# 111 unread products of the identity between the steps of a fixed TensorE order, in a Mamba, attention and gated-FFN tower on one core

## The chip, the core and the metric

The kernel runs on one core of a Trainium2 chip. The core has TensorE (PE in the profile, with its weight loads as PEld), VectorE (DVE), ScalarE (ACT), GpSimd (POOL) and SyncE (SP), which here only starts transfers. The metric is the device time of one execution in microseconds. The kernel before took 393.94 us as the median of three runs (392.65 to 394.93).

## What is computed

Sixteen sequences of 128 tokens go through an embedding of width 192, two Mamba layers, one attention layer and one feed-forward layer, each with a residual sum. Cut to its core:

```python
x = emb[input_ids]
for i in range(2):                       # Mamba, inner width 384, 16 states
    xr, res = split(rmsnorm(x) @ in_proj_w[i])
    xr = silu(causal_conv4(xr) + conv_b[i])
    dt, Bm, Cm = split(xr @ x_proj_w[i])
    delta = softplus(dt @ dt_proj_w[i] + dt_proj_b[i])
    y = selective_scan(xr, delta, -exp(A_log[i]), Bm, Cm, D[i])
    x = x + (y * silu(res)) @ out_proj_w[i]
q, k, v = split(layernorm(x) @ w_qkv)    # 12 heads of 16
attn = relu(1 + qk + qk ** 2 / 2); attn = attn / sum(attn)
x = x + (attn @ v) @ w_proj + b_proj
up, gate = split(quant(rmsnorm(layernorm(x))) @ ternary(w_in).T)
x = x + quant(rmsnorm(silu(gate) * up)) @ ternary(w_out).T
```

## The kernel before

**Staging.** The two Mamba layers are cut into eight chunks j = 0 to 7: four groups of four sequences, and two layers. Each chunk has 512 tokens and three channel blocks c of 128. Chunk 4 is the first of layer 1. Attention and the feed-forward part run by sequence, s = 0 to 15.

**Order.** Nothing is scheduled at run time. Each engine has a list of calls, written out by hand, and walks through it in order. Semaphores tie the lists together: a call waits for the count that its data or its bank needs. On TensorE the list of calls begins behind the helper functions, with turn_in(0, 0).

**TensorE's helpers.** turn_in(j, k) (L972) transposes the normalised input of a chunk, eight 128x128 pieces in two calls. project_in(j, q) (L983) and project_rest(j, q) (L989, L991) form the input projection, in three parts q, which ScalarE's first_tap and silu_gate_in (L374) read. project_x(j) (L998) gives the rows of dt, B and C, which ScalarE's take_xp copies to dbl (L328). project_steps(j) (L1005) gives the step sizes, which ScalarE reads for the softplus. spread_b(j) (L1010) and spread_cg(j) (L1016, L1018) spread B, C and their product over the partitions, for VectorE. project_out(j, b) (L1065) is the output projection, which VectorE's add_h (L2335) adds to h. Behind them come turn_x, project_qk, project_v, scores(s) (L1115), values(s) (L1127), turn_sums(s) (L1135, L1138), turn_attention and project. In the feed-forward part turn_input (L1160), project_up (L1167), turn_hidden(s) (L1174) and project_down(s) (L1181) stand. project_down(s) waits for ScalarE's copy of the turned tile (take_hidden, L534), and VectorE's add_ffn(s) (L2459) waits for it and makes the last sum of a sequence, which SP stores.

**Flags.** Whether a chunk's states need the long form is decided at run time. VectorE counts and writes a flag (L2328); every engine reads it, TensorE in states_pe(j) (L1021 and after), and takes a branch. In this run every chunk takes the short branch, in which states_pe only raises a semaphore. ScalarE's take_xp(j) waits for that semaphore of chunk j - 2.

**Banks.** PSUM has eight banks of 128x512 float32, and tables at the head of the file say which bank each call writes. A product that nobody reads has to find its bank free, so it may stand only behind the count that says that the last reader of the bank is done.

**What is not used.** The helper keep_clock(n, b) (L965) is defined in the kernel before and called nowhere:

```python
def keep_clock(n, b):
    for _ in range(n):
        nc.tensor.matmul(bank[:, b, 0:P], ident[:, :], ident[:, :], start=True, stop=True)
```

## Time and profile before

| | |
|---|---|
| median of the runs | 393.94 us |
| the profiled execution | 396.22 us |
| its span, first to last instruction | 394.2 us |
| mean granted TensorE clock | 0.908 of full |
| PE busy | 325.8 us (83%) |
| DVE busy | 294.0 us (75%) |
| ACT busy | 272.4 us (69%) |
| POOL busy | 235.3 us (60%) |

The profile is of one execution, which has its own time. The busy shares are means over stages that differ: the Mamba layers fill about the first 236 us, attention and the feed-forward part the rest. The clock is given as a share of full: 1.00 is 2.4 GHz and 0.50 is 1.2 GHz. A plain float32 product shows as two MATMUL records, a transpose as one.

### The profile page before, as it was taken

To read this page: it belongs to the slowest core of one execution; us is meant where nothing else is said; L and a number is where in the kernel's file an instruction comes from. 1 tells how busy PE (TensorE), PEld (TensorE's weight loads), DVE (VectorE), ACT (ScalarE), POOL (GpSimd) and SP (SyncE) were. 2 spreads that over 40 slices of the span, in tenths; PEclk is the share of its full clock that TensorE was granted. 3 is DMA by queue.
4 is the path that set the end of the run, shared out by engine and by line. 5 is a ranking of instruction groups with operands and counts; after the bars stand their busy time and mean duration, and the time that the engine had idled before them with its cause. 6 is when DMAs were issued, how large, how long until landed. Compare 5 with 4: busy or idle time off the path is not lost. (4 is left out here: it accounts for less than half of the span.)

```text
span 394.2 us, 6391 instructions
## 1 busy us (share of the span) xinstructions
PE 325.8 (83%) x1794; PEld 188.7 (48%) x1794; DVE 294.0 (75%) x636; ACT 272.4 (69%) x552; POOL 235.3 (60%) x316
## 2 busy tenths in 40 slices
PE   0199965768978899998989889988998899899955
PEld 0143422254425534364335558646765646477633
DVE  3019999899899899999998959941365737467874
ACT  2459999696688998799876964353555547566852
POOL 6751168578819459296392691760134836678893
PEclk9999995959899998998979969998999969899976
DMA  6891000000000000000000000000000000000111
GB/s 151 150 274 23 1 2 0 2 1 0 2 1 1 2 0 2 2 1 0 2 1 0 1 3 2 0 2 2 0 2 2 0 2 1 2 12 10 32 60 50
DMA packets 7134, 7.87 MB, mean 20 GB/s; under 512 B 1643, under 2 KB 6138, under 8 KB 7098
## 3 DMA queue, kind: packets, MB, share of 16 engines
q1 hardware_dynamic: 5464, 5.71, 4.9%
q0 software_dynamic: 768, 1.57, 2.8%
q8 instruction: 15, 0.25, 0.2%
q10 hardware_dynamic: 866, 0.17, 0.2%
q14 instruction: 21, 0.17, 0.2%
HBM read 5.87 MB, written 1.57 MB: 19 GB/s over the span
## 5 line engine op out<-in xcount | busy, mean ns | idle before, releaser
L983 PE MATMUL bank<-ring,win 128*128 128x512 f32 x96 | 53.4, 690 | 7.4 <-DVE dmin L2248 3.3
L1856 POOL TENSOR_TENSOR arena<-arena 128x512 f32<-128x512 f32 x24 | 34.0, 1428 | 39.9 <-DVE arena L2282 25.9
L2239 DVE SCALAR_TENSOR_TENSOR pair<-bank,cw,pair 128x508 f32<-128x508 f32 (+2 forms) x72 | 49.8, 733 | 5.8 <-issue 4.7
L1838 POOL TENSOR_TENSOR arena<-arena,dl 128x512 f32<-128x512 f32 x24 | 31.9, 1332 | 22.9 <-DVE dl L2231 22.6
L1065 PE MATMUL bank<-wout,pair 128*128 128x192 f32 x192 | 37.7, 352 | 3.3 <-ACT ring L382 3.3
L480 ACT ACTIVATE du<-bank 128x512 f32<-128x512 f32 x48 | 25.3, 597 | 19.9 <-PE bank L1115 17.4
L1065 PEld LDWEIGHTS bank<-wout,pair 128*128 128x128 f32 x192 | 34.1, 206 | 9.5 <-ACT ring L382 3.7
L1844 POOL TENSOR_TENSOR du<-dl,pair 128x512 f32<-128x512 f32 x24 | 33.1, 1383 | 8.8 <-DVE dmin L2248 8.8
L983 PEld LDWEIGHTS bank<-ring,win 128*128 128x128 f32 x96 | 19.0, 216 | 35.0 <-issue 18.8
L2269 DVE TENSOR_TENSOR_SCAN arena<-arena 128x512 f32<-128x512 f32 x24 | 34.8, 1461 | 0.3
L972 PE MATMUL bank<-ident,ring 128*128 128x128 f32 x64 | 11.7, 330 | 23.8 <-ACT ring L409 19.0
L1850 POOL TENSOR_TENSOR pair<-pair,arena 128x512 f32<-128x512 f32 x24 | 31.2, 1316 | 0.0
L989 PE MATMUL bank<-ring,win_rest 64*128 64x512 f32 x48 | 26.3, 641 | 0.0
L991 PE MATMUL bank<-ring,win_rest 64*128 64x512 f32 x48 | 26.3, 641 | 0.0
L998 PE MATMUL bank<-pair,wx 128*125 128x512 f32 x48 | 24.0, 639 | 1.3 <-issue 1.3
L972 PEld LDWEIGHTS bank<-ident,ring 128*128 128x128 f32 x64 | 8.9, 170 | 30.1 <-issue 23.5
L1890 POOL TENSOR_TENSOR pair<-pair,gout 128x512 f32<-128x512 f32 x16 | 20.5, 1285 | 1.8 <-PE bank L1174 1.1
L335 ACT ACTIVATE pair<-bank,cb,cw 128x512 f32<-128x512 f32 x24 | 18.5, 787 | 3.8 <-PE bank L991 2.3
L1833 POOL TENSOR_TENSOR rstd<-ms,neg_half 128x4 f32<-128x4 f32 x8 | 9.2, 1147 | 19.7 <-DVE ms L2219 16.5
L1167 PE MATMUL bank<-wq,arena 96*128 96x512 bf16 x64 | 18.6, 397 | 1.4 <-ACT arena L507 1.4
L2263 DVE TENSOR_TENSOR arena<-du,bank 128x512 f32<-128x512 f32 x24 | 16.2, 681 | 4.3 <-PE bank L1010 2.8
L2277 DVE TENSOR_TENSOR arena<-du,bank 128x512 f32<-128x512 f32 x24 | 16.3, 678 | 4.1 <-POOL pair L1850 3.5
(177 smaller groups left out, 887.1 us busy)
## 6 DMA issues: line engine op xcount, KB each, us to landing
out<-h SPq DMA_DIRECT2D x16, 96.0 KB, 1.6
win<-in_w SPq DMA_DIRECT2D x2, 384.0 KB
arena<-ffn_in_t SPq DMA_DIRECT2D x1, 768.0 KB
wout<-out_w SPq DMA_DIRECT2D x2, 288.0 KB
win_rest<-in_w SPq DMA_DIRECT2D x2, 192.0 KB
arena<-ffn_out_t SPq DMA_DIRECT2D x1, 384.0 KB
wa<-w_qkv SPq DMA_DIRECT2D x1, 384.0 KB
h<-emb,idx POOLq DMA_INDIRECT x16
```

The costliest lines, as they stand in the source:

```text
L480: nc.scalar.activation(sq[s % 2][:, r, :, :], bank[:, SC_BANKS[s][r], :].rearrange("p (j n) -> p j n", j=JH), ACT.Square, scale=HD ** -0.5 ...
L983: nc.tensor.matmul(bank[:, IN_BANKS[j][m], :], win[:, j // NG, m * P:(m + 1) * P], xtr[:, j % 2, i, :], start=True, stop=False)
L989: nc.tensor.matmul(bank[:, IN_BANKS[j][2 * q], :], rest[64:P, :], xtr[64:P, j % 2, 1, :], start=False, stop=True).then_inc(x_ready if 2 * ...
L991: nc.tensor.matmul(bank[:, IN_BANKS[j][2 * q + 1], :], rest[0:64, :], xtr[0:64, j % 2, 0, :], start=False, stop=True).then_inc(x_ready if ...
L998: last = nc.tensor.matmul(bank[0:XM, XP_BANKS[j], :], wx[:, j // NG, c, :], xc[:, j % NG, c, :], start=(c == 0), stop=(c == CI - 1))
L1065: last = nc.tensor.matmul(bank[:, O_BANKS[j][b], i * D:(i + 1) * D], xc[:, j % NG, c, t0:t0 + LEN], wout[:, j // NG, c, :], start=(c == 0) ...
L1838: nc.gpsimd.tensor_tensor(relu_s[:, c, :], relu_s[:, c, :], dl[:, j % NG, c, :], ALU.subtract).then_inc(rest_done, 1)
L1844: nc.gpsimd.tensor_tensor(du[:, g, c, :], dl[:, g, c, :], xc[:, g, c, :], ALU.mult).then_inc(du_ready, 1)
L1850: nc.gpsimd.tensor_tensor(xc[:, j % NG, c, :], sz[:, j % NG, c, :], yv[:, c, :], ALU.mult).then_inc(gated, 1)
L1856: nc.gpsimd.tensor_tensor(yv[:, c, :], yv[:, c, :], bx[:, c, :], ALU.add).then_inc(yv_done, 1)
L2239: nc.vector.scalar_tensor_tensor(acc, seqs(bank[:, IN_BANKS[j][c], :])[:, :, 0:LEN - tap], cw[:, j // NG, c, TAPS - 1 - tap:TAPS - tap], a ...
L2269: nc.vector.tensor_tensor_scan(bx[:, c, :], da[:, c, :], bx[:, c, :], 0.0, ALU.mult, ALU.add).then_inc(scan_done, 1)
```

## The change

keep_clock is called at 19 places of TensorE's list, with 111 products in all. The numbers of products are 7, 1, 1, 1, 4, 6, 10, 4, 4, 6, 8, 2, 1, 2, 4, 4, 3, 25 and 18. Each writes 128 columns of a bank that no one reads before it is written again. Before most of them stands the wait that says the bank is free. Some of these waits stood a few calls further on before and are moved ahead, others are new. No call changes its place against the others, on any engine.

```diff
             turn_in(0, 0)
             turn_in(0, 1)
+            keep_clock(7, 2)
             pe.wait_ge(xt_ready, 2)
             project_in(0, 0)
...
             project_in(1, 1)
+            pe.wait_ge(conv[0], 3)
+            keep_clock(1, 1)
             project_rest(1, 1)
             pe.wait_ge(sz_ready, 2)
-            pe.wait_ge(conv[0], 3)
             project_in(1, 2)
...
             project_in(2, 0)
+            pe.wait_ge(sz_ready, 6)
+            keep_clock(1, 1)
             project_rest(2, 0)
-            pe.wait_ge(sz_ready, 6)
             project_x(1)
...
             project_in(2, 1)
+            pe.wait_ge(conv[0], 9)
+            keep_clock(1, 6)
             project_rest(2, 1)
+            pe.wait_ge(delta_ready, 1)
+            keep_clock(4, 0)
             pe.wait_ge(conv[1], 9)
-            pe.wait_ge(delta_ready, 1)
-            pe.wait_ge(conv[0], 9)
             project_steps(1)
...
             project_in(2, 2)
+            pe.wait_ge(delta_ready, 5)
+            keep_clock(6, 0)
             pe.wait_ge(bx_ready, 3)
             turn_in(3, 0)
...
             states_pe(0)
             pe.wait_ge(flag_ready, 1)
+            keep_clock(10, 4)
             pe.wait_ge(xt_ready, 7)
             pe.wait_ge(p_done, 3)
             project_steps(2)
...
             states_pe(1)
+            pe.wait_ge(delta_ready, 8)
+            keep_clock(4, 1)
             pe.wait_ge(p_done, 6)
             turn_in(4, 0)
...
             states_pe(4)
+            pe.wait_ge(p_done, 13)
+            pe.wait_ge(p_done, 14)
             pe.wait_ge(p_done, 15)
+            keep_clock(4, 3)
             pe.wait_ge(t_ready, 15)
             pe.wait_ge(sz_ready, 18)
             project_steps(5)
...
             project_out(4, 1)
+            pe.wait_ge(sz_ready, 20)
+            keep_clock(6, 0)
             pe.wait_ge(h_added, 9)
             turn_in(7, 0)
             pe.wait_ge(h_added, 10)
             turn_in(7, 1)
-            pe.wait_ge(sz_ready, 20)
             project_x(6)
+            pe.wait_ge(delta_ready, 18)
+            keep_clock(8, 5)
             pe.wait_ge(t_ready, 18)
             pe.wait_ge(bx_ready, 18)
-            pe.wait_ge(delta_ready, 18)
             project_steps(6)
...
             project_rest(7, 0)
+            pe.wait_ge(sz_ready, 21)
+            keep_clock(2, 4)
             pe.wait_ge(flag_ready, 6)
-            pe.wait_ge(sz_ready, 21)
             project_in(7, 1)
+            pe.wait_ge(p_done, 16)
+            pe.wait_ge(p_done, 17)
+            pe.wait_ge(p_done, 18)
+            keep_clock(1, 1)
             project_rest(7, 1)
             states_pe(5)
             pe.wait_ge(delta_ready, 19)
-            pe.wait_ge(p_done, 18)
+            keep_clock(2, 3)
             project_in(7, 2)
...
             states_pe(6)
             pe.wait_ge(k_out, 2)
+            keep_clock(4, 5)
             pe.wait_ge(q_out, 4)
             pe.wait_ge(p_done, 21)
             scores(0)
...
             turn_hidden(10)
+            pe.wait_ge(y_done, 14)
+            keep_clock(4, 2)
             pe.wait_ge(qxt_ready, 16)
             project_up(15, 1)
             pe.wait_ge(y_done, 15)
             project_up(15, 0)
+            keep_clock(3, 2)
             pe.wait_ge(yt_ready, 11)
             project_down(10)
             pe.wait_ge(sg_ready, 16)
             turn_hidden(11)
+            pe.wait_ge(h_out, 9)
+            keep_clock(25, 1)
             pe.wait_ge(yt_ready, 12)
             project_down(11)
             pe.wait_ge(h_out, 11)
             turn_hidden(12)
+            pe.wait_ge(y_done, 16)
+            keep_clock(18, 0)
             pe.wait_ge(yt_ready, 13)
             turn_hidden(13)
```

On TensorE, at the end of its list, these rows stand in the kernel before. L1160 and L1174 are turn_input and turn_hidden, L1167 is project_up and L1181 project_down:

```order
L1160 MATMUL bank<-ident,ring 96x128 x2
L1174 MATMUL bank<-ident,pair 128x128 x4
L1167 MATMUL bank<-wq,arena 128x512 x4
L1181 MATMUL bank<-wq,arena 128x192 x4
L1174 MATMUL bank<-ident,pair 128x128 x4
L1181 MATMUL bank<-wq,arena 128x192 x4
L1174 MATMUL bank<-ident,pair 128x128 x8
L1181 MATMUL bank<-wq,arena 128x192 x4
```

At the same place of the changed kernel:

```order
L1160 MATMUL bank<-ident,ring 96x128 x2
L1174 MATMUL bank<-ident,pair 128x128 x4
L967 MATMUL bank<-ident 128x128 x4
L1167 MATMUL bank<-wq,arena 128x512 x4
L967 MATMUL bank<-ident 128x128 x3
L1181 MATMUL bank<-wq,arena 128x192 x4
L1174 MATMUL bank<-ident,pair 128x128 x4
L967 MATMUL bank<-ident 128x128 x25
L1181 MATMUL bank<-wq,arena 128x192 x4
L1174 MATMUL bank<-ident,pair 128x128 x4
L967 MATMUL bank<-ident 128x128 x18
L1174 MATMUL bank<-ident,pair 128x128 x4
```

The 25 products stand between turn_hidden(11) and project_down(11), and the 18 part turn_hidden(12) from turn_hidden(13), which were one row of eight transposes.

On TensorE, behind the branch of states_pe(1) and before turn_in(4, 0) (L972) and project_in(3, 2) (L983):

```order
 L1043 COMPARE_AND_BRANCH
 L1026 UNCONDITIONAL_BRANCH
+L967 MATMUL bank<-ident 128x128 x4
 L972 MATMUL bank<-ident,ring 128x128 x4
 L983 MATMUL bank<-ring,win 128x512 x2
```

The four products come after the branch, so the transposes stand one row further from it. The same form stands behind states_pe(0), (4), (5) and (6).

## Rows read from the trace of the kernel before

**Rows 1.** The page's slices: busy tenths of the span's 40 equal parts.
```profile
PE   0199965768978899998989889988998899899955
...
DVE  3019999899899899999998959941365737467874
...
PEclk9999995959899998998979969998999969899976
```

**Rows 2.** Waits of DVE, 28 to 232 us: total, times, longest.
```profile
DVE arena L2263 <- PE bank L1010: 2.8, 2, 1.8
DVE h L2335 <- PE bank L1065: 2.2, 2, 1.6
```

**Rows 3.** Timeline of PE in attention: start us, us, line, operation, idle before.
```profile
238.60 0.83 PE L1138 MATMUL bank<-ident,arena 128*128 128x128 f32 x6
239.27 0.81 PE L1135 MATMUL bank<-dl,ones 128*128 128x384 f32 x2
```

**Rows 4.** Timeline of PE at the kernel's end.
```profile
377.23 1.02 PE L1167 MATMUL bank<-wq,arena 96*128 96x512 bf16 x4 [0.95 <-ACT arena L507]
378.95 0.49 PE L1181 MATMUL bank<-wq,arena 128*128 128x192 bf16 x4 [0.70 <-ACT arena L534]
379.74 1.09 PE L1174 MATMUL bank<-ident,pair 128*128 128x128 f32 x4 [0.29 <-DVE pair L2453]
383.24 0.80 PE L1181 MATMUL bank<-wq,arena 128*128 128x192 bf16 x4 [2.41 <-ACT arena L534]
...
386.92 1.09 PE L1174 MATMUL bank<-ident,pair 128*128 128x128 f32 x4 [2.03 <-DVE pair L2453]
...
389.77 0.60 PE L1174 MATMUL bank<-ident,pair 128*128 128x128 f32 x4
```

**Rows 5.** The last piece of the chain that ended last.
```profile
391.77 0.42 DVE h L2459
```

**Rows 6.** Timeline at the start, PE and ACT.
```profile
20.00 5.84 PE L983 MATMUL bank<-ring,win 128*128 128x512 f32 x8 [0.82 <-ACT ring L382]
...
26.97 2.12 ACT L335 ACTIVATE pair<-bank,cb,cw 128x512 f32<-128x512 f32 x3 [1.20 <-PE bank L991]
...
28.62 3.68 PE L983 MATMUL bank<-ring,win 128*128 128x512 f32 x8
```

**Rows 7.** Timeline of PE behind states_pe(1).
```profile
99.21 0.87 PE L972 MATMUL bank<-ident,ring 128*128 128x128 f32 x4 [2.12 <-issue]
```

**Rows 8.** Timeline of PE and ACT behind states_pe(0).
```profile
77.54 0.69 ACT L328 ACTIVATE dbl<-bank,one_rows 125x512 f32<-125x512 f32 x1 [2.21 <-PEq L1025]
...
78.37 1.53 PE L1005 MATMUL bank<-dbl,wdt 29*128 29x512 f32 x6 [2.65 <-ACT dbl L328]
...
84.21 6.62 PE L1065 MATMUL bank<-wout,pair 128*128 128x192 f32 x24 [3.26 <-ACT ring L382]
...
85.52 1.18 ACT L364 ACTIVATE bank<-bank 128x512 f32<-128x512 f32 x2 [0.87 <-DVE dl L2231]
```

**Rows 9.** Timeline of PE behind states_pe(6), scores(0) and scores(1).
```profile
225.28 1.14 PE L1115 MATMUL bank<-pair 32*128 32x256 f32 x12 [0.26 <-issue]
228.22 1.20 PE L1115 MATMUL bank<-pair 32*128 32x256 f32 x12 [1.80 <-ACT du L480]
```

**Rows 10.** Timeline of PE in chunks 6 and 7.
```profile
183.48 1.12 PE L972 MATMUL bank<-ident,ring 128*128 128x128 f32 x8 [1.97 <-DVE h L2335]
184.44 4.43 PE L998 MATMUL bank<-pair,wx 128*125 128x512 f32 x6
189.74 1.13 PE L1005 MATMUL bank<-dbl,wdt 29*128 29x512 f32 x6 [0.87 <-ACT dbl L328]
```

**Rows 11.** Stretches: length, busy PE, PEld, DVE, ACT, POOL, clock, DMA share, GB/s.
```profile
79.00:89.20 10.20, 6.94 (x26) 5.71 (x21) 10.13 (x16) 8.89 (x17) 7.98 (x6) 0.50 0.00 1
...
229.20:236.00 6.80, 6.67 (x68) 3.82 (x64) 3.22 (x8) 4.15 (x8) 6.80 (x6) 0.50 0.01 4
379.40:389.60 10.20, 5.46 (x27) 4.52 (x27) 7.03 (x18) 2.74 (x6) 8.52 (x19) 0.50 0.13 41
```

More of the change, by code:

```diff
@@ L1245, in _ @@
             count_short(0)
-            pe.wait_ge(delta_ready, 5)
             project_x(2)
@@ L1277, in _ @@
             pe.wait_ge(flag_ready, 2)
-            pe.wait_ge(delta_ready, 8)
             project_in(3, 2)
@@ L1794, in _ @@
             project_down(12)
-            pe.wait_ge(y_done, 16)
             turn_hidden(14)
```

## The prediction

> **What bounds the kernel now.** I read the view of the slices first. The reader is to see two halves [rows 1]: up to slice 24 (some 236 us) VectorE stands at 9 nearly everywhere, and TensorE has open slices; from there TensorE stands at 8 or 9 and VectorE falls back. The clock line shows 5 in five slices and 6 to 8 in several more. So a slow TensorE costs time at full rate only in the second half; in the first it costs time where VectorE waits for TensorE. Those waits are few: of 204 us, VectorE waited 2.8 us for the spread of B (L1010) and 2.2 us for the output projection (L1065), in two waits each [rows 2]. The third place is the end, where TensorE, ScalarE and VectorE alternate and each instruction is on the path [rows 4]. The profiled execution took 396.22 us, with a span of 394.2; the median shown is 393.94. I work out differences in the execution and add them to the median.
>
> **The price of one product.** keep_clock issues plain float32 products of 128x128. The nearest row is the one of turn_sums, three products of the same shape that show as six records: from its start at 238.60 to the next line's at 239.27 are 0.67 us, so 0.111 a record and 0.222 us a product at the full clock [rows 3]. Four float32 transposes show as four records: 0.60 us at the full clock and 1.09 at the half [rows 4], not far from double. So I take a record at half clock as 0.222 and a product as 0.44 us.
>
> **The end of the kernel.** This is the heaviest term. turn_hidden(11) starts at 379.74, and project_down(11) starts at 383.24 after 2.41 idle; turn_hidden(13) starts at 386.92 after 2.03 idle [rows 4]. The change puts 25 products into the first gap and 18 into the second: 5.55 and 4.00 us at the full clock against 4.44 us of idle in all. The waits put ahead of them (h_out 9, y_done 16) do not hold them back: VectorE runs add_ffn(8) and hidden(15) well before, since the square of tile 15 and the copy of tile 11 on ScalarE, for which project_down(11) waited, come after hidden(15). So the products start as soon as TensorE gets to them. The 4 and 3 products a little earlier (0.9 and 0.7 us) fit the gaps there of 0.95 and 0.70 [rows 4], and I cost them at nothing. With these, I expect the clock, which fell at about 379.4, to stay full. Then the walk, in times of before: turn_hidden(11) is issued by 380.2; 25 products to 385.7; project_down(11) and turn_hidden(12), 0.35 + 0.45, to 386.5; 18 products to 390.5. The rounds of the last hidden tiles, which were what TensorE waited for at 386.92, are then all done: project_down(11) is 2.5 late and VectorE's add behind it too, but its rounds for 13, 14 and 15 follow by about 389.7. From turn_hidden(13) to the end of the last add were 5.27 us (386.92 to 392.19), mostly at half clock. At full clock: 0.45 for turn_hidden(13) (four records of 0.11), 0.35 for project_down(12) (0.49 with its tail), 0.45 for turn_hidden(14), 0.8 for the wait for ScalarE's copy of tile 13 and project_down(13), 0.45 for turn_hidden(15), 0.7 and 0.2 of latency for the copy of tile 15, and 0.49 and 0.42 for the last product and add [rows 4, 5]: some 4.2 us. End at 394.7 against 392.19: **+2.6**. Who waits: SP's last stores, one for one. Without the gain in clock it would be +3.6. If the clock does not hold and the 25 start at half rate, say thirteen of them, it is 13 x 0.22 = 2.9 more.
>
> **The start.** Seven products stand between turn_in(0,1) and project_in(0,0). In between TensorE was idle 0.82 us, and it worked below the full rate then: the eight records of project_in took 5.84 us, 0.73 each, against 3.68 for eight at 28.62 [rows 6], though the clock column, which starts with its first event, says full. ScalarE's first tap waited 1.20 us for the products behind them [rows 6], and VectorE starts behind it, so this is on the path. At half rate the seven are 3.1 us, 2.3 more than the gap. The activity may raise the clock earlier: by one early change, project_in ends 0.6 before; with none, 0.9 after. I take -0.3, nearer the first, since the gap was the one break in TensorE's work there.
>
> **After the flags.** Three of the groups stand behind states_pe, where TensorE's sequencer reads a flag and branches. The idle time is spent in that read, and the products come after it. So they fill nothing there.
> - Before turn_in(4,0): 2.12 idle, put down to "issue" [rows 7]. Four products are 0.9 us. Behind stands spread_b(2), for which VectorE waited the longest of its waits for that line, 1.8 us [rows 2]; this passes on in full: **+0.9**. If the clock held, project_in(3,2) would give back 1.4, so -0.5; at half clock +1.7.
> - Before project_steps(2): ten products are 2.2 us, and TensorE waited 2.65 us there for ScalarE's dbl [rows 8], and ScalarE itself had waited for TensorE's branch until 77.54 [rows 8]. Only 0.8 lies between branch and steps, so project_steps(2) comes 1.4 late. ScalarE has 0.87 to spare behind it, at 85.52 [rows 8], so **+0.5**. Between -0.3 (the output projection at 84.21, 6.62 us at half clock, runs faster and the shorter of the two waits for it, 0.6, goes [rows 2, 8]) and +1.5.
> - Before scores(0): 0.26 idle [rows 9] against 0.9 for four products: **+0.65**. Here TensorE bounds from now on. The real gap, 1.80 us, lies behind scores(0), where ScalarE squares [rows 9], and gets no product.
>
> **Chunk 6 and 7.** Six products before turn_in(7,0) fit the 1.97 idle, with 0.6 to spare [rows 10]. There the clock fell right behind, and project_x(6) took 4.43 us, nearly all at half rate [rows 10]: at full rate 1.6 come back, somewhat under the 2.2 that half of it would be. The eight products before project_steps(6) are 1.8 us in a gap of 0.87 [rows 10], so 0.9 is taken again: **-0.6**; +0.9 if the clock falls all the same. Five more products (1.1 us) stand in front of and between the projections of chunk 7, at 193 to 197, with no idle time; the break before spread_b(6), in which the clock fell again, takes them up. They may keep the clock for spread, turn_x and project_out(5,0), behind which VectorE had its longest wait for the output projection, 1.6 us [rows 2]. Only part of this break is filled, so I count **-0.3**, between 0 and -1.6.
>
> **What else moves.** Waits were taken forward so that a bank is free: conv[0] 3 and 9, sz_ready 6 and 20, delta_ready 1, 5, 8, 18, 19. The one with work behind it is delta_ready 5 with six products before turn_in(3,0), where TensorE had no gap: project_rest(2,2) and the gate's silu on ScalarE come 1.3 late, but ScalarE waits 2.21 us a little later for the flag's branch, which covers it [rows 8]. conv[0] 9 holds project_rest(2,1) for some 0.5 us, ahead of 1.35 idle. The single products there are 0.2 each beside the same covers. Four before project_steps(5), behind a branch too, delay it by some 0.7, and ScalarE loads a table and takes a tap before it needs it. All at nothing; up to +1.0 if these covers fail.
>
> **Sum:** -0.3 + 0.9 + 0.5 + 0.65 - 0.6 - 0.3 + 2.6 = +3.45 us. 393.94 + 3.45 = **397.4 us**.
>
> **Rivals.**
> 1. The clock holds nearly everywhere beside the products, and TensorE's faster work carries. The places are the half-clock stretches of 79 to 89, 229 to 236 and 379 to 389 [rows 11] and the waits of VectorE [rows 2]. For: the falls follow breaks such as those of 2.65, 2.12, 1.97 and 1.80 us [rows 7 to 10]. Against: the products at scores(0) and turn_in(4,0) are not in the break. Price: the 6.7 us of TensorE at half clock in 229 to 236, where it bounds, give 3.3; VectorE's waits for L1065 give 2.2, and that at spread_b(2) 1.4 [rows 2]: -6.9, against 2.6 at the end and 2.2 in products: -2.1, and with 0.6 at the start -2.7, so 391.2. It decides for faster once more than 4.8 us come back; the stretch of scores alone is most of that. 8%. The Trainium skill ("TensorE: Matmul & The Clock Gate", section "Terms") reckons the penalty of throttled time as that time x (1 - K/N), so half of it. By that rule the 27.2 us of the three stretches would be worth 13.6 us, and the time 380; the rows speak against it, since VectorE was busy 10.1 of the 10.2 us from 79 to 89 [rows 11], and I leave it 1 of the 8%.
> 2. The 25 products run largely at half rate and the clock follows late: +2.9 on the sum, or the covers above fail too: 400.0 to 401. 12%.
> 3. A product costs what a transpose does, one record, 0.111 us. 25 are 2.8 against 2.41, 18 are 2.0 against 2.03: the end costs +0.4 less 1.0 of regained clock, and the places behind the flags half: some -0.3 in all, 393.6. Against: turn_sums shows two records a product [rows 3]. Or the early terms turn out as gains of 1.5 to 2: then some 394 to 395.5. Together 18%.
> 4. The forecast, 395.5 to 399.5: 62%.
>
> **Numbers.** The range reaches from 393.5 to 400.3: it leaves out rival 1 and half of rival 2. Over 0.5% (2 us, about what a measurement can tell) means above 395.9 or below 392.0: slower 0.70 (the forecast less its lowest part, and rival 2), faster 0.08, same 0.22.
>
> **What would show it.** Right: the 25 and 18 rows of L967 last some 5.5 and 4 us; project_down(11) follows them without a wait, and so does turn_hidden(13); the clock is full from 379 on and the last add ends 2 to 3 us later, counted from turn_hidden(11). At turn_in(4,0) some 2 us of idle stand ahead of the products still. Wrong: a wait for y_rounded between the 18 products and turn_hidden(13), as then the price is off; or no half clock in 229 to 236.

## The result and the profile after

The changed kernel takes 398.06 us (median of four runs, 397.26 to 399.79) against 393.84 for the kernel before beside it. The ratio is 1.0114, with a 95% interval of 1.0069 to 1.0158: 4.5 us more, with bounds of 2.7 and 6.2. The forecast was 3.45 more, 397.4. In comparisons of single terms below, I use ratios to the kernel before; 0.001 is 0.39 us. A ratio leaves out executions that are more than 1.5% above the fastest of their kernel.

The page of the changed kernel: span, busy times, and the same slices as [rows 1].

```profile
span 395.8 us, 6828 instructions
...
PE 340.0 (86%) x2016; PEld 211.9 (54%) x2016; DVE 295.3 (75%) x636; ACT 272.1 (69%) x552; POOL 235.8 (60%) x316
...
PE   0299985969879788999989979988998899899996
...
PEclk9999995978898999999998969999899989999999
```

TensorE is busy 14 us longer than before (340.0 against 325.8) and its mean clock rose from 0.908 to 0.948, while VectorE, ScalarE and GpSimd did the same work as before. A better clock and a longer time stand side by side; the rest of this text is about why. The profiled execution took 397.81 us, only 1.6 more than the one profiled before (396.22). That pair understates the difference, since that execution of before was longer than all four of its timed runs (392.65 to 394.93).

**The end.** TensorE's timeline (start us, us, line, operation, records, idle before), which answers to [rows 4]:

```profile
378.72 0.63 PE L1174 MATMUL bank<-ident,pair 128*128 128x128 f32 x4 [0.29 <-DVE pair L2478]
379.19 5.75 PE L967 MATMUL bank<-ident 128*128 128x128 f32 x50
384.77 0.49 PE L1181 MATMUL bank<-wq,arena 128*128 128x192 bf16 x4
385.10 0.60 PE L1174 MATMUL bank<-ident,pair 128*128 128x128 f32 x4
385.54 4.18 PE L967 MATMUL bank<-ident 128*128 128x128 f32 x36
389.56 0.60 PE L1174 MATMUL bank<-ident,pair 128*128 128x128 f32 x4
...
392.82 0.49 PE L1181 MATMUL bank<-wq,arena 128*128 128x192 bf16 x4 [0.54 <-ACT arena L534]
```

The 25 products are 50 records in 5.75 us, the 18 are 36 in 4.18, and what follows each has no idle time in front. TensorE has become the bound of this piece. From turn_hidden(11) at 378.72 to the end of the last add (393.35 and 0.42 us, the same add as in [rows 5]) are 15.05 us; before they were 12.45, from 379.74 to 392.19 [rows 4, 5]. Four transposes now take 0.60 us where most took 1.09. Counted from start to start, the 25 take 5.58 us (379.19 to 384.77) and the 18 take 4.02, so 0.223 us a product; the lengths of the rows, 5.75 and 4.18, contain the tail of the last product.

**Behind the flags.** The same timeline behind states_pe(0), (1) and (6), which answers to [rows 7 to 9]:

```profile
77.83 2.50 PE L967 MATMUL bank<-ident 128*128 128x128 f32 x20
80.26 1.13 PE L1005 MATMUL bank<-dbl,wdt 29*128 29x512 f32 x6
...
85.74 7.03 PE L1065 MATMUL bank<-wout,pair 128*128 128x192 f32 x24 [3.76 <-ACT ring L382]
...
100.89 1.25 PE L967 MATMUL bank<-ident 128*128 128x128 f32 x8 [1.87 <-issue]
101.94 1.06 PE L972 MATMUL bank<-ident,ring 128*128 128x128 f32 x4
102.79 3.10 PE L983 MATMUL bank<-ring,win 128*128 128x512 f32 x4
...
226.37 1.16 PE L967 MATMUL bank<-ident 128*128 128x128 f32 x8
227.46 1.14 PE L1115 MATMUL bank<-pair 32*128 32x256 f32 x12
...
230.42 1.14 PE L1115 MATMUL bank<-pair 32*128 32x256 f32 x12 [1.82 <-ACT du L480]
```

Before turn_in(4,0) the idle time is still there (1.87 us, put down to "issue"), and the four products come behind it, as extra. Before scores(0) they are 1.1 us in front of a call that had waited 0.26. The real gap, 1.82 us before scores(1), is untouched. VectorE's waits for TensorE, of the stretch that [rows 2] shows (L2288 and L2360 are L2263 and L2335 of before), grew in sum. The first for the output projection went from 0.66 to 1.80 us; the second, for a later chunk, shrank from 1.56 to 1.30.

```profile
DVE arena L2288 <- PE bank L1010: 4.2, 2, 2.5
DVE h L2360 <- PE bank L1065: 3.1, 2, 1.8
```

**Chunk 6.** Here the products are in the gap of [rows 10]:

```profile
183.78 1.50 PE L967 MATMUL bank<-ident 128*128 128x128 f32 x12
185.91 1.12 PE L972 MATMUL bank<-ident,ring 128*128 128x128 f32 x8 [0.62 <-DVE h L2360]
186.86 2.74 PE L998 MATMUL bank<-pair,wx 128*125 128x512 f32 x6
189.44 1.95 PE L967 MATMUL bank<-ident 128*128 128x128 f32 x16
191.32 1.14 PE L1005 MATMUL bank<-dbl,wdt 29*128 29x512 f32 x6
```

0.62 us of the wait for h are left over, so nothing is pushed back, and project_x(6) takes 2.74 where it took 4.43 [rows 10]. That this gain is owed to the products is not shown: in the trace of waits_only (below), which issues no product, the call takes 2.74 too, behind 2.00 us idle.

```profile
182.70 2.74 PE L998 MATMUL bank<-pair,wx 128*125 128x512 f32 x6
```

The eight that follow overrun the gap of 0.87 us, as costed.

**The clock.** Stretches as in [rows 11]: length, busy time of each engine, clock (third from the end). The stretch of scores is still at half, and the last 16.6 us are at nearly full clock:

```profile
231.50:238.30 6.80, 6.54 (x68) 3.72 (x67) 2.99 (x2) 4.27 (x9) 6.80 (x5) 0.50 0.01 4
379.40:396.00 16.60, 13.27 (x122) 12.57 (x120) 7.17 (x19) 4.05 (x7) 7.32 (x18) 0.98 0.14 42
```

**Where the time came in.** I set VectorE's instructions of the two traces side by side, one by one. The changed kernel is 0.47 us later at 61 us, 0.8 at 85, 1.9 at 91 (behind the wait for the output projection of chunk 0) and 2.6 at 106 (behind spread_b(2)). It then falls back to 1.7 at 196 and 1.4 at 212, is 2.1 later at 233, just behind scores(0), and takes its last 2.6 in the end. Between 288 and 349 it goes from 2.3 later to 1.0 earlier, where the change has no product: the half clock there held 3.4 us from 317 where it had held 6.8 from 314, and one of 3.4 at 342 was absent. The trace of waits_only (below), which has no product, shows the falls of the changed kernel there, 3.4 us from 313 and none at 342, so I count nothing of this to the change. The same caution holds for the first half: VectorE of waits_only, with no product at all, is 2.35 us earlier than that of the kernel before at 104 us, where half clock is absent at 99.5, and 5.1 earlier at the end. One pair of traces is therefore no measure of a term below some 2 us.

### The profile page after: what moved, and what is told of

Its sections match the earlier page's. It is cut to its first block and busy times, and to the rows that moved or that the text cites. A ratio compares the mean times of both kernels' runs of the same rounds, so it can differ in the third digit from the quotient of the medians.

```text
span 395.8 us, 6828 instructions
## 1 busy us (share of the span) xinstructions
PE 340.0 (86%) x2016; PEld 211.9 (54%) x2016; DVE 295.3 (75%) x636; ACT 272.1 (69%) x552; POOL 235.8 (60%) x316
## 3 DMA queue, kind: packets, MB, share of 16 engines
q0 software_dynamic: 768, 1.57, 2.8%
HBM read 5.87 MB, written 1.57 MB: 19 GB/s over the span
## 5 line engine op out<-in xcount | busy, mean ns | idle before, releaser
L983 PE MATMUL bank<-ring,win 128*128 128x512 f32 x96 | 51.2, 665 | 7.0 <-DVE dmin L2273 3.3
L1065 PE MATMUL bank<-wout,pair 128*128 128x192 f32 x192 | 39.2, 361 | 3.9 <-ACT ring L382 3.8
L1065 PEld LDWEIGHTS bank<-wout,pair 128*128 128x128 f32 x192 | 35.4, 212 | 10.0 <-issue 4.1
L967 PEld LDWEIGHTS bank<-ident 128*128 128x128 f32 x222 | 29.3, 207 | 11.1 <-issue 6.9
L983 PEld LDWEIGHTS bank<-ring,win 128*128 128x128 f32 x96 | 18.4, 209 | 31.3 <-issue 19.8
L967 PE MATMUL bank<-ident 128*128 128x128 f32 x222 | 31.3, 295 | 2.1 <-issue 1.9
L1875 POOL TENSOR_TENSOR pair<-pair,arena 128x512 f32<-128x512 f32 x24 | 33.0, 1390 | 0.0
L972 PE MATMUL bank<-ident,ring 128*128 128x128 f32 x64 | 10.5, 306 | 20.3 <-ACT ring L409 19.0
L998 PE MATMUL bank<-pair,wx 128*125 128x512 f32 x48 | 22.2, 599 | 1.3 <-issue 1.3
L972 PEld LDWEIGHTS bank<-ident,ring 128*128 128x128 f32 x64 | 8.0, 156 | 24.1 <-issue 19.5
L2288 DVE TENSOR_TENSOR arena<-du,bank 128x512 f32<-128x512 f32 x24 | 16.1, 678 | 5.7 <-PE bank L1010 4.2
```

Of the source, the lines that this page charges most:

```text
L983: nc.tensor.matmul(bank[:, IN_BANKS[j][m], :], win[:, j // NG, m * P:(m + 1) * P], xtr[:, j % 2, i, :], start=True, stop=False)
L1065: last = nc.tensor.matmul(bank[:, O_BANKS[j][b], i * D:(i + 1) * D], xc[:, j % NG, c, t0:t0 + LEN], wout[:, j // NG, c, :], start=(c == 0) ...
L1875: nc.gpsimd.tensor_tensor(xc[:, j % NG, c, :], sz[:, j % NG, c, :], yv[:, c, :], ALU.mult).then_inc(gated, 1)
```

## The experiments

Each kernel ran against the kernel before on the same chip. There were three groups of kernels, each on a chip of its own: waits_only, tail_only, no_tail and no_behind_flags; tail_fit, ahead_of_flags, scores_gap and in_the_gaps; and the remaining four. The tables give the ratio with its 95% interval, the span and mean clock of the profiled execution, and the **last piece**, from turn_hidden(11) to the end of the last add.

### Taking the change apart

Theory: three lots of products carry it, the 25 and 18 at the end, the five groups behind the flags (10, 4, 4, 2, 4), and the other 44, which together pay a little. Rival: the moved waits cost, or the shared effect of the clock does.

waits_only keeps every wait of the change and no product:

```diff
             pe.wait_ge(h_out, 9)
-            keep_clock(25, 1)
...
             pe.wait_ge(y_done, 16)
-            keep_clock(18, 0)
```

> The changed kernel with all 111 products left out and only its moved and added waits kept. Theory (the products cost TensorE's time where its idle time is shorter than they are, the waits cost nothing): within 0.5 us of the kernel before, ratio 0.999 to 1.001. Rival (the waits taken forward hold back project_rest and what stands behind it): 1 us or more slower. Second rival (the clock's luck decides): no statement, anywhere within 1.5 us.

tail_only keeps, with the waits, only the last four groups:

```diff
-            keep_clock(7, 2)
...
-            keep_clock(4, 5)
...
             keep_clock(4, 2)
...
             keep_clock(3, 2)
...
             keep_clock(25, 1)
...
             keep_clock(18, 0)
```

> Only the last four groups of products (4, 3, 25 and 18) are kept, with all waits of the change. Theory: TensorE becomes the bound of the last 13 us; +2.6 us against the kernel before, ratio 1.0066; in the profile from the start of turn_hidden(11) to the end of the last add some 15.0 us, where 12.45 stood. Rival (the cost sits in the Mamba layers): +0 to +0.5.

no_tail is the changed kernel without the last two:

```diff
-            keep_clock(25, 1)
...
-            keep_clock(18, 0)
```

> The changed kernel without the groups of 25 and 18; the other 68 products stay. Theory: 2.6 us less than the changed kernel, so +1.0 to +1.8 against the kernel before (ratio 1.003 to 1.0045); the piece from turn_hidden(11) to the last add takes 11.5 to 12.45 us, less than before if the 4 and 3 products keep the clock up. Rival: as slow as the changed kernel.

no_behind_flags is the changed kernel without the five groups behind branches:

```diff
-            keep_clock(10, 4)
...
-            keep_clock(4, 1)
...
-            keep_clock(4, 3)
...
-            keep_clock(2, 3)
...
-            keep_clock(4, 5)
```

> The changed kernel without the five groups that stand behind a read flag (10, 4, 4, 2 and 4 products). Theory: they stand behind the idle time and not in it, and cost 0.9 at turn_in(4,0), 0.5 to 1.4 at project_steps(2) and 0.65 at scores(0): about 2.0 to 2.4 us less than the changed kernel, so +1.5 to +2.2 against the kernel before (ratio 1.004 to 1.0055). Rival (what they do to the clock outweighs their time): no less than the changed kernel, or more.

neither leaves both out, so 44 products stay (the two edits above in one):

> The changed kernel without the five groups behind the flags and without the 25 and 18 at the end; 44 products stay. Theory (the flags' groups and the end are the whole cost): no slower than the kernel before, ratio 0.997 to 1.001. Rival (the products in the dense stretches of chunks 1, 2, 6 and 7 and at the start cost too): 1 us slower or more.

| kernel | ratio | 95% | span, clock | last piece |
|---|---|---|---|---|
| waits_only | 0.9996 | 0.9973 to 1.0019 | 389.1, 0.924 | 12.59 |
| tail_only | 1.0023 | 0.9997 to 1.0048 | 393.9, 0.935 | 15.05 |
| no_tail | 1.0078 | 1.0046 to 1.0110 | 397.0, 0.927 | 13.37 |
| no_behind_flags | 1.0017 | 0.9993 to 1.0042 | 391.6, 0.948 | 15.05 |
| neither | 0.9957 | 0.9927 to 0.9988 | 400.9, 0.905 | 12.94 |

The profiled execution of neither took 402.77 us, while its other twelve took 390.13 to 393.84, so its last two columns do not stand for the kernel.

The moved waits cost nothing that can be measured. Four of the kernels make a square, in us against the kernel before (394 times the ratio less one):

| | without 25 and 18 | with them |
|---|---|---|
| without the groups behind flags | -1.7 | +0.7 |
| with them | +3.1 | +4.5 |

The end costs 2.4 in the upper row and 1.4 in the lower. The groups behind flags cost 4.8 in the left column and 3.8 in the right. Each of the four has an interval of 1 to 2 us to either side, so that the two columns differ is not shown. The kernel neither comes from another chip than no_tail and no_behind_flags. A third pair, tail_only less waits_only, prices the last four groups at 1.1 us.

The other products can be priced within one group of kernels: no_behind_flags is tail_only with 37 products more, those at the start and in chunks 1, 2, 6 and 7. Their ratios, 1.0017 and 1.0023, and medians, 394.62 and 394.55 us, are the same. So these 37 cost nothing and bring nothing that can be told, within some 1.4 us.

Two of the traces also show where the groups behind the flags cost. VectorE of the changed kernel, set against VectorE of no_behind_flags, is 0.8 us later at 86 us, 2.6 at 92.8 (behind the wait for the output projection of chunk 0) and 4.9 at 108.5 (behind spread_b(2)); from 160 to 212 it is 3.8 to 4.1 later, 5.3 at 233, and 4.2 from 239 to the end. The whole cost of this pair arises before 110 us, at the first two flags, and nothing is lost in attention. no_tail against waits_only shows the same steps: 2.5 us by 92 and 4.7 by 108. The rows of no_behind_flags, against the output projection at 85.74, turn_in(4,0) at 101.94 and the wait of 2.5 us above:

```profile
84.35 5.78 PE L1065 MATMUL bank<-wout,pair 128*128 128x192 f32 x24 [3.96 <-ACT ring L382]
...
98.40 0.63 PE L972 MATMUL bank<-ident,ring 128*128 128x128 f32 x4 [2.00 <-issue]
98.86 1.88 PE L983 MATMUL bank<-ring,win 128*128 128x512 f32 x4
...
103.56 0.69 DVE L2283 TENSOR_TENSOR arena<-du,bank 128x512 f32<-128x512 f32 x1 [0.25 <-PE bank L1010]
```

At both places the clock adds to the products' own time. The output projection takes 7.03 us where it takes 5.78 here, and the first part of project_in(3,2) 3.10, in a stretch at 0.50 from 101.8 to 105.2, where it takes 1.88 at full clock. Whether the four products brought that second fall is not shown: the kernel before has it too, at 99.5, and so has tail_only, while waits_only has none there.

The last piece explains part of the end's two prices: without the products it is 12.5 us in waits_only but 13.37 in no_tail, because the half clock lasted longer in it there. What the products add to the piece is therefore 2.5 or 1.7, as the execution falls. tail_only came out at +0.9 where I had expected the whole 2.6. Its last piece is 15.05, exactly as expected; what gave back the rest lies before turn_hidden(11), and no run isolates it.

no_tail was a miss of mine. I had written +1.0 to 1.8 and it was +3.1, and this is the first sign that the groups behind the flags had been costed too low. no_behind_flags missed too, on the other side (+1.5 to +2.2 expected, +0.7 measured).

### The end, with products that fit

The timeline gives a product 0.22 to 0.23 us. If the 25 and 18 cost because they overrun gaps of 2.41 and 2.03 us [rows 4], then 10 and 8 should pay.

```diff
             pe.wait_ge(h_out, 9)
-            keep_clock(25, 1)
+            keep_clock(10, 1)
...
             pe.wait_ge(y_done, 16)
-            keep_clock(18, 0)
+            keep_clock(8, 0)
```

The rest is as in tail_only.

> The waits of the change, and at the end of the kernel groups of 4, 3, 10 and 8 products instead of 4, 3, 25 and 18; no others. At 0.222 us each, 10 and 8 are 2.2 and 1.8 us, in gaps of 2.41 and 2.03. Theory (the cost at the end is products beyond the gap, and the clock they hold is worth 1 us): the piece from turn_hidden(11) to the last add takes 11.2 to 11.6 us, against 12.45 before and 15.05 with 25 and 18; ratio 0.997 to 0.999 against the kernel before, 2.5 to 3.5 us faster than with 25 and 18. Rival (a product costs what a transpose does, so 25 and 18 fit as well): no difference from the run with 25 and 18.

The ratio is 0.9952 (0.9924 to 0.9981), a little better than expected; span 390.3, clock 0.934, last piece 11.58. TensorE's timeline of its end:

```profile
376.72 0.63 PE L1174 MATMUL bank<-ident,pair 128*128 128x128 f32 x4 [0.29 <-DVE pair L2463]
377.19 2.40 PE L967 MATMUL bank<-ident 128*128 128x128 f32 x20
380.22 0.49 PE L1181 MATMUL bank<-wq,arena 128*128 128x192 bf16 x4 [0.64 <-ACT arena L534]
...
380.99 1.95 PE L967 MATMUL bank<-ident 128*128 128x128 f32 x16
383.90 0.63 PE L1174 MATMUL bank<-ident,pair 128*128 128x128 f32 x4 [0.96 <-DVE pair L2463]
```

And the same end in waits_only, without products:

```profile
374.46 1.09 PE L1174 MATMUL bank<-ident,pair 128*128 128x128 f32 x4 [0.30 <-DVE pair L2459]
377.96 0.80 PE L1181 MATMUL bank<-wq,arena 128*128 128x192 bf16 x4 [2.41 <-ACT arena L534]
...
381.64 1.08 PE L1174 MATMUL bank<-ident,pair 128*128 128x128 f32 x4 [2.03 <-DVE pair L2459]
```

The waits for ScalarE and VectorE are back as the bound, but short (0.64 and 0.96), so no product is on the path, and the transposes, here 0.63, stay at the full clock's duration. From turn_hidden(11) to turn_hidden(13) are 7.18 us in both: the gain lies behind, where the clock is full (3.46 us from turn_hidden(13) to the start of the last project_down, against 4.47). 25 products fewer at the two places are 7 parts in 1000, or 2.8 us, against tail_only (each ratio from its own chip), and the two last pieces differ by 3.47.

### Ahead of a flag or behind it

The claim that products behind a flag fill nothing, because the idle time is spent in the read, has a counterpart: products ahead of the read should hide in it.

```diff
+            pe.wait_ge(xt_ready, 7)
+            keep_clock(8, 1)
             states_pe(0)
             pe.wait_ge(flag_ready, 1)
...
-            states_pe(1)
             pe.wait_ge(delta_ready, 8)
+            keep_clock(6, 1)
+            states_pe(1)
```

The edit is against waits_only, so no other product is issued.

> The waits of the change, and products at two flags only, ahead of the flag's read and not behind it: eight before states_pe(0), six before states_pe(1). Theory (behind a flag the idle time is already over, ahead of it the products fill it): turn_in(4,0) starts no more than 2.2 us behind the last projection as before, the products hide, the clock holds in one of the two stretches behind, and VectorE's waits for L1065 and L1010 shrink: 0 to 1.5 us faster than the kernel before. Rival (the read of the flag waits until TensorE's products are through, so products push it wherever they stand): 1.5 to 3 us slower.

The ratio is 0.9986 (0.9954 to 1.0017), span 390.1, clock 0.924, last piece 12.56. TensorE's timeline:

```profile
76.70 2.05 PE L967 MATMUL bank<-ident 128*128 128x128 f32 x16
...
96.93 1.61 PE L967 MATMUL bank<-ident 128*128 128x128 f32 x12
98.90 0.63 PE L972 MATMUL bank<-ident,ring 128*128 128x128 f32 x4 [0.37 <-issue]
```

The six stand in the former break, of which 0.37 us are left, and turn_in(4,0) starts at 98.90 where it started at 99.21 [rows 7]. In waits_only, without products, it starts at 98.32 behind 1.96 us of idle. Four products cost 1.1 us behind the branch, and six are hidden ahead of it. The rival, by which products push the read wherever they stand, is out: 1.5 to 3 us slower was its price. The kernel gains nothing measurable either.

Two kernels price the groups behind the branch alone. ten_at_steps2 has every wait and only the ten (the cuts here are against waits_only):

```diff
             states_pe(0)
             pe.wait_ge(flag_ready, 1)
+            keep_clock(10, 4)
             pe.wait_ge(xt_ready, 7)
```

> The waits of the change, and only the ten products before project_steps(2), behind the read of flag 0. The prediction priced them at +0.5. Its changed trace shows VectorE's wait for the output projection of chunk 0 at 1.80 us where 0.66 stood, and its shift growing there by 1.9 in all. Theory now: +1.5 to +2.0 us against the kernel before, ratio 1.004 to 1.005. Rival (the price of the prediction): +0.5, ratio 1.001.

fours_behind_flags has only the four before turn_in(4,0) and the four before scores(0):

```diff
             pe.wait_ge(delta_ready, 8)
+            keep_clock(4, 1)
             pe.wait_ge(p_done, 6)
...
             pe.wait_ge(k_out, 2)
+            keep_clock(4, 5)
             pe.wait_ge(q_out, 4)
```

> The waits of the change, and only the four products before turn_in(4,0) and the four before scores(0), both behind a flag. Theory: 0.9 and 0.65, each on the path: +1.5 us, ratio 1.004. Rival (one of the two is taken up by a later wait): +0.9 or less.

| kernel | ratio | 95% | span, clock | last piece |
|---|---|---|---|---|
| ten_at_steps2 | 1.0040 | 1.0006 to 1.0074 | 392.9, 0.916 | 12.54 |
| fours_behind_flags | 1.0147 | 1.0095 to 1.0200 | 398.8, 0.914 | 13.01 |

The ten cost 1.6 us by the ratio, with bounds of 0.2 and 2.9, so the ratio alone does not exclude the 0.5 of the prediction. The traces speak more clearly: from 75 to 92 us VectorE falls back by 1.4 to 2.8 us against the kernel before in the three that have the ten there (the changed kernel, no_tail, ten_at_steps2), and by 0.6 at most in each of the others, without them. TensorE's and VectorE's timeline of ten_at_steps2, to be held against [rows 8]:

```profile
77.22 4.13 PE L967 MATMUL bank<-ident 128*128 128x128 f32 x20 [1.00 <-issue]
...
86.77 6.42 PE L1065 MATMUL bank<-wout,pair 128*128 128x192 f32 x24 [3.76 <-ACT ring L382]
...
93.22 0.56 DVE L2342 TENSOR_TENSOR h<-h,bank 128x384 f32<-128x384 f32 x1 [1.20 <-PE bank L1065]
```

Here the ten ran at half clock (4.13 us), and the output projection starts at 86.77, where it started at 84.21. VectorE, which I had not counted on this path, waits 1.20 us for it instead of 0.66 in the kernel before.

The fours cost 5.8 us (3.7 to 7.9, from six executions), far above what their places can show: in the changed kernel four products take 1.05 us before turn_in(4,0) and 1.09 before scores(0). It is also more than the +3.1 of no_tail, which has the same fours and 60 products more. In the profiled execution VectorE is 1.7 us later than that of the kernel before at 98 us, ahead of the first product, 2.3 at 233 and 4.5 at the end. The last part came where the kernel has no product, with stretches of half clock and TensorE fully busy, of which these are two:

```profile
268.40:271.80 3.40, 3.40 (x16) 2.93 (x18) 1.23 (x5) 1.00 (x3) 0.30 (x1) 0.51 0.00 0
...
343.40:350.20 6.80, 6.78 (x30) 4.25 (x30) 2.59 (x7) 3.04 (x6) 3.06 (x8) 0.51 0.00 0
```

Four transposes take 1.09 us at half clock and 0.60 at full, so by an estimate such a stretch of 3.4 us costs 1.5 where TensorE is the bound. That the fours bring these stretches about is not shown. The long profiled execution of neither, which has no product behind a flag, has stretches of the same lengths at nearly the same places (from 267, 304, 321 and 345 us, against 268, 302, 319 and 343 here). The first of them:

```profile
267.00:273.80 6.80, 6.48 (x26) 5.38 (x26) 2.52 (x9) 1.75 (x4) 1.78 (x4) 0.50 0.01 4
```

And the changed kernel has the same fours, with fewer such stretches. So the 5.8 us are no price of the fours, and their cause stays open.

### The gap that the change left open

scores_gap puts six products into the 1.80 us before scores(1) [rows 9], and none elsewhere. Theory: the clock holds over 229 to 236, where TensorE bounds, and some 3 us come back.

```diff
             pe.wait_ge(v_out, 2)
+            keep_clock(6, 1)
             scores(1)
```

> The waits of the change, and one group of six products between scores(0) and scores(1), in the gap of 1.80 us where TensorE waits for ScalarE's squares. Theory: the 1.3 us fit, the clock holds from 229 to 236, where TensorE bounds, and 2 to 3 us come back; ratio 0.993 to 0.996. Rival (the clock falls all the same, as the score products do not count for it): within 0.5 us of the kernel before; or the wait for v_out 2 comes later than I read it, and it is 0.5 slower.

The ratio is 1.0050 (1.0017 to 1.0083), span 393.0, clock 0.917, last piece 13.35. TensorE's timeline and the stretches:

```profile
226.76 1.61 PE L967 MATMUL bank<-ident 128*128 128x128 f32 x12 [0.30 <-DVE dmin L2255]
...
231.26 1.14 PE L1115 MATMUL bank<-pair 32*128 32x256 f32 x12 [0.98 <-ACT du L480]
```

```profile
229.00:236.00 7.00, 6.02 (x86) 3.81 (x83) 4.30 (x11) 4.71 (x10) 7.00 (x6) 1.00 0.00 1
...
377.10:390.80 13.70, 8.65 (x43) 6.54 (x41) 8.30 (x21) 4.16 (x8) 8.61 (x19) 0.51 0.16 50
```

The first half of the theory held. The clock stands at 1.00 from 229 to 236, scores(2) takes 1.14 us where it takes 2.08 in waits_only, and VectorE, set against waits_only, gained 2.5 us over it (the profiled execution of waits_only was its fastest). The second half fell: the half clock came back at 298, 339 and for 13.7 us at 377 (10.2 before [rows 11]), and the kernel is 2 us slower. The mean clocks of its executions, 0.916 to 0.926, are hardly above those of the kernel before beside it, 0.902 to 0.924. That the six products moved the falls from one place to others is an argument from one trace and not shown.

### All gaps together

in_the_gaps joins what fitted: 8 and 6 products ahead of the flags, 6 before turn_in(7,0), 3 (not 8) before project_steps(6), 6 before scores(1), and 4, 3, 10 and 8 at the end, 54 in all. gaps_but_scores is the same without the six before scores(1). Against waits_only:

```diff
+            pe.wait_ge(xt_ready, 7)
+            keep_clock(8, 1)
             states_pe(0)
...
-            states_pe(1)
             pe.wait_ge(delta_ready, 8)
+            keep_clock(6, 1)
+            states_pe(1)
...
+            keep_clock(6, 0)
             pe.wait_ge(h_added, 9)
             turn_in(7, 0)
...
+            keep_clock(3, 5)
             pe.wait_ge(t_ready, 18)
...
+            keep_clock(4, 2)
...
+            keep_clock(3, 2)
...
+            keep_clock(10, 1)
...
+            keep_clock(8, 0)
```

> All groups that fit an idle time of TensorE together: 8 and 6 ahead of the first two flags, 6 before turn_in(7,0), 3 before project_steps(6), 6 between the first two scores, and 4, 3, 10 and 8 at the end. Theory: the gains add: 4 to 7 us faster than the kernel before, ratio 0.982 to 0.990, mean granted clock 0.95 or more. Rival (the clock is no bound of the first half, and the falls only move to the next break): 0 to 2 us faster.

> As in_the_gaps, but without the six products between scores(0) and scores(1): 8 and 6 ahead of the flags, 6 before turn_in(7,0), 3 before project_steps(6), and 4, 3, 10 and 8 at the end. Theory (the scores group moves the clock's falls into the attention's later breaks, and makes the executions spread): executions lie close together again, within 3 us, and the median is 2 to 3 us below the kernel before, ratio 0.992 to 0.995. Rival (the spread comes from the groups ahead of the flags): a spread of 8 us or more again.

| kernel | median | ratio | 95% | span, clock | last piece |
|---|---|---|---|---|---|
| in_the_gaps | 394.39 | 0.9944 | 0.9895 to 0.9993 | 389.3, 0.942 | 11.59 |
| gaps_but_scores | 390.73 | 0.9938 | 0.9905 to 0.9971 | 388.8, 0.943 | 11.57 |

gaps_but_scores beats both kernels: 2.4 us less than before, some 7 less than the changed kernel, with 48 products and not 111. But tail_fit, with the last 25 of these 48 alone, came to 0.9952 (0.9924 to 0.9981), and the last pieces of the two are 11.57 and 11.58 us. So the products that fit at the end are enough to explain the gain, and that the other 23 bring anything is not shown.

The ratio of in_the_gaps is not to be trusted: its twelve runs go from 388.08 to 400.32 us, and the ratio rests on the shorter six; what made the others longer can't be told. By its median, 394.39 against 393.65, it is no faster than before, so the 4 to 7 us expected of it did not come: the gains do not add. Twelve runs of gaps_but_scores stay between 388.68 and 394.09, wider than the 3 us expected, while its median came as expected. The two kernels ran on different chips. The six products before scores(1) bring nothing that can be seen, here as alone.

## Why the prediction was right, point by point

**The total.** +3.45 was forecast and +4.5 measured, inside the interval, and for the reason named: products that overrun their gaps on a path where TensorE is late. The size is in part luck. Of the terms, the flags were priced too low by some 2 us, the end came out lower than forecast on the whole kernel, and the gains of the start and of chunks 6 and 7 are not shown.

**The end, +2.6: right in the trace, high for the kernel.** Its price per product, 0.222 us, was 0.223 measured from start to start; the clock held, as forecast; no wait stood between the 18 and turn_hidden(13). The piece from turn_hidden(13) to the last add was forecast at some 4.2 us (its nine terms add up to 4.3) and took 4.21. The last piece grew by 2.60 in the traces. On the whole kernel the end is worth 2.4 in the square's upper row, 1.4 in the lower and 1.1 between waits_only and tail_only. The single number from one trace was thus the upper end. Part of the reason is that the piece without products lasts 12.5 to 13.4 us.

**Behind the flags, +2.05: the step that was mis-sized.** It measured 3.8 to 4.8 for all five groups, of which the prediction put two at nothing. That the idle time stays and the products come behind it was right (1.87 us before the products at turn_in(4,0)), and the step at scores(0) is 0.65 against the kernel before and 0.5 against no_behind_flags, where 0.65 was forecast. Against no_behind_flags, the cost is 2.6 us by 92.8, where 0.5 was forecast, and 2.3 more by 108.5, where 0.9 was forecast. The +0.5 for the ten products rested on ScalarE's spare 0.87 us [rows 8]. I followed ScalarE and not TensorE's own next calls, whose output projection moved from 84.21 to 85.74 and made VectorE wait 1.80 us where it had waited 0.66:

```profile
92.80 0.55 DVE L2360 TENSOR_TENSOR h<-h,bank 128x384 f32<-128x384 f32 x1 [1.80 <-PE bank L1065]
```

And the 0.9 at turn_in(4,0) counted the products alone. Of the 1.4 that the prediction named as the worth of the clock in project_in(3,2), 1.2 is the difference in this pair, 3.10 us against 1.88. Against the kernel before, which had the half clock there too, the step from 91 to 106 us is 0.7.

**The start, -0.3: not shown.** The seven products ran at half rate (3.19 us, forecast 3.1) and project_in(0,0) took 4.27 where it took 5.84 [rows 6]. It started 1.97 us later (21.97 against 20.00) and lasted 1.57 less, so ScalarE's first tap came 0.4 late (27.37 against 26.97 [rows 6]):

```profile
18.98 3.19 PE L967 MATMUL bank<-ident 128*128 128x128 f32 x14
21.97 4.27 PE L983 MATMUL bank<-ring,win 128*128 128x512 f32 x8
...
27.37 2.11 ACT L335 ACTIVATE pair<-bank,cb,cw 128x512 f32<-128x512 f32 x3 [0.94 <-PE bank L991]
```

In all traces, project_in(0,0) lasts 3.60 to 4.27 us with the seven and 5.06 to 6.53 without, so that they speed it up is shown. From the first turn_in to the first tap it takes 9.2 to 10.1 us in the four traces with them and 9.2 to 10.4 in the ten without, so the two effects cancel and the sign is not settled.

**Chunks 6 and 7, -0.9: the number met, the cause not shown.** The shift of VectorE falls by 0.7 between 187 and 194 where -0.6 was forecast (its own terms, -1.6 and +0.9, give -0.7), and 0.62 us of the gap were to spare (0.6 forecast). But the half clock of 184.8 to 188.2, whose absence gives this gain, is absent in waits_only and tail_only as well, where VectorE gains the same 0.73 there without a product. Every trace without this half clock shows that 0.73, with these groups or not. From 180 to 215 us the four traces with all of them gain 0.3 to 1.2 us on the kernel before, and the seven with none gain 0.5 to 0.7. All 44 products outside the flags and the last two groups measured -1.7 (-2.9 to -0.5), where -1.2 was forecast with the start, but 37 of them, compared on one chip, measured -0.2.

**The waits, 0: right**, by waits_only (0.9996, within 0.9 us).

**Readings.** The clock line of [rows 1] shows 5 in two slices, not in five, and VectorE stands at 9 up to slice 26 rather than 24. Rival 3 adds up to about -0.8 by its own terms, not -0.3. None of these carries the forecast.

**The rivals.** The clock did not hold everywhere; 231.5 to 238.3 stood at half, as the forecast had it. The rule of the Trainium skill by which half the throttled time is lost ("TensorE: Matmul & The Clock Gate", section "Terms"), which I had left 1 in 100, did not come true: the clock of the span rose by 0.04 of full and the time by 1.1%, with 14 us of products added. A product showed two records, so rival 3 fell.

**What stays open.** Why the half clock falls where it does, behind the first flags and in attention, and so why scores_gap and fours_behind_flags were 2 and 5.8 us slower than the kernel before. Whether the four products before turn_in(4,0) brought the fall behind them. And what gives back over 1 us of tail_only's 2.6 ahead of its last piece.

## What to carry to other kernels

An unread product is free only in a wait whose releaser is another engine and comes later than the product ends; measure the gap, divide by the price (here 0.22 us), and leave some of it over. Idle time ahead of an instruction is not always in front of what is written there: where it is the read of a flag, the product must go ahead of the read. And judge by the time: a clock that is better by 0.04 came with a slower kernel, so try each group with and without the rest. Before a gain is put down to a group, look for it in a trace that lacks the group: here a full-speed project_x(6) stood there as well.

## What was not expected of the hardware

The granted clock differs between executions of one and the same kernel: in the runs of the kernel before beside the experiments its mean lay between 0.902 (398.44 us) and 0.924 (391.15 us), and longer runs mostly went with the lower clock. waits_only and the kernel before, without a product in either, differ by 2.35 us at 104 us. The spread of a kernel differs too: 12 us over the runs of in_the_gaps, 5.4 over those of gaps_but_scores and 5.1 over those of scores_gap, which has the same six products before scores(1) as in_the_gaps; so those six alone do not explain it.
